# The head products of a group norm as two rounded passes, in newly ordered steps of a two-layer fp32 kernel

## The reference

```
xa = _ln(x, ln1_w, ln1_b)
sx = concatenate([state[:, 1:2] - xa[:, :1], xa[:, :-1] - xa[:, 1:]], axis=1)
xxx = tanh((xa + sx * maa_x) @ maa_w1) ...      # five mixes of xa and sx
w = exp(-exp(time_decay + tanh(xw @ td_w1) @ td_w2))
r, k, v = xr @ Wr.T, xk @ Wk.T, xv @ Wv.T;  g = silu(xg @ Wg.T)
for each token:                                  # the recurrence
    a = k_t[..., :, None] * v_t[..., None, :]
    out = einsum('bhi,bhij->bhj', r_t, u * a + s)
    s = a + w_t[..., :, None] * s
og = out.reshape(b, l, h, s_)                    # group norm over each head's 16 channels
m = og.mean(-1, keepdims=True)
va = ((og - m) ** 2).mean(-1, keepdims=True)
og = ((og - m) / sqrt(va + 1e-05)).reshape(b, l, e) * gn_w + gn_b
x1 = x + og * g @ Wo.T
xc = _ln(x1, ln2_w, ln2_b)
...
return x1 + rr * (kk @ Wfv.T)                    # rr = sigmoid(xr2 @ Wfr.T), kk = relu(xk2 @ Wfk.T)^2
```

## Time and profile before

| | us |
|---|---|
| median of 3 runs | 1405.7 |
| lowest and highest | 1401.32, 1408.68 |
| the profiled execution, its own time | 1402.65 |
| its span, from the first to the last instruction | 1400.8 |
| PE busy | 1331.3 (95% of the span) |
| DVE busy | 928.5 (66%) |
| ACT busy | 734.7 (52%) |
| POOL busy | 489.8 (35%) |

### The profile page before, as it was taken

How to read it: one execution, slowest core, us unless ns; L and a number is a source line. 1 busy time by engine, 2 the same in 40 slices (tenths; PEclk the granted TensorE clock), 3 DMA queues, 4 the chain that set the end, 5 groups by cost and what they waited for, 6 DMA issues and landing times.

```text
span 1400.8 us, 42823 instructions
## 1 busy us (share of the span) xinstructions
PE 1331.3 (95%) x17120; PEld 937.6 (67%) x17120; DVE 928.5 (66%) x2431; ACT 734.7 (52%) x1772; POOL 489.8 (35%) x550
## 2 busy tenths in 40 slices
PE   6999999999999999897899999999999999999977
PEld 5777777777777777666566666766676667666624
DVE  3555555555555555547677877787888888887862
ACT  4776677767667667632425453445345434444332
POOL 3222111222222222113346445543555345534540
PEclk9999999999999999988999999999999999999979
DMA  7333222222222223113000010001010110010000
GB/s 228 99 106 106 93 75 63 74 73 71 61 76 74 75 69 101 54 57 122 22 21 14 23 28 21 15 22 28 22 27 9 28 27 22 10 26 22 15 14 14
DMA packets 39529, 73.70 MB, mean 53 GB/s; under 512 B 17797, under 2 KB 20485, under 8 KB 37829
## 3 DMA queue, kind: packets, MB, share of 16 engines
q1 hardware_dynamic: 39365, 71.24, 17.2%
HBM read 60.24 MB, written 7.57 MB: 48 GB/s over the span
## 4 chain that ended last, share of the span: by engine, by line
PE 82%; DVE 8%; issue 6%; DMA 2%; ACT 1%; SPq 1%; POOL 0%; DVEq 0%; ACTq 0%; POOLq 0%
PE b_bank L1831 18%; PE b_bank L1837 12%; PE ring_bank L703 7%; PE ring_bank L704 6%; PE ring_bank L705 6%; PE av_bank L789 4%; PE b_bank L1945 4%; PE score_banks L762 4%; DVE probs L450 3%; PE b_bank L1982 3%; PE score_banks L749 3%; PE b_bank L1971 2%; PE b_bank L1885 2%; DVE probsT L467 2%; PE av_bank L775 2%
## 5 line engine op out<-in xcount | busy, mean ns | idle before, releaser
L1126 POOL TENSOR_TENSOR rst<-rp,st 128x448 f32<-128x448 f32 x192 | 209.7, 1115 | 55.9 <-DVE st L1349 53.9
L450 DVE CUSTOM_DVE_ANT_0 probs<-score_banks,unmask 112x375 f32<-112x375 f32 x256 | 124.8, 544 | 93.0 <-issue 93.0
L595 ACT ACTIVATE probs<-probs,least_inv 112x375 f32<-112x375 f32 x256 | 152.4, 606 | 32.5 <-DVE least_inv L450 32.5
L467 DVE SCALAR_TENSOR_TENSOR probsT<-score_banks,least_cols 125x448 f32<-125x448 f32 x192 | 107.9, 617 | 53.9 <-PE score_banks L762 51.7
L610 ACT ACTIVATE probsT<-probsT,key_mask 125x448 f32<-125x448 f32 x192 | 114.5, 661 | 47.4 <-DVE probsT L467 47.2
L1118 POOL TENSOR_TENSOR xm<-mixed,xa 128x448 f32<-128x448 f32 x80 | 88.0, 1102 | 145.3 <-DVE mixed L1278 140.0
L340 POOL TENSOR_TENSOR aT_lo<-whole,aT_hi 128x375 fp32r<-128x375 f32 x64 | 59.0, 921 | 152.3 <-ACT whole L576 150.2
L375 POOL TENSOR_TENSOR ctx_rstd<-ctx_var_eps,a_eps_exp 125x3 f32<-125x3 f32 x16 | 13.8, 865 | 272.6 <-DVE ctx_var_eps L423 272.6
L703 PE MATMUL ring_bank<-aT_hi,wk_lo 128*128 128x376 f32 x256 | 91.2, 356 | 0.2 <-issue 0.2
L1628 ACT COPY key<-b_bank 128x448 f32<-128x448 f32 x16 | 8.5, 533 | 148.4 <-PE b_bank L1831 148.4
L704 PE MATMUL ring_bank<-aT_lo,wk_hi 128*128 128x376 f32 x256 | 85.5, 334 | 0.0
(11 more groups left out here) (183 smaller groups left out, 3109.0 us busy)
## 6 DMA issues: line engine op xcount, KB each, us to landing
least_cols<-values_of_two_batches SPq DMA_DIRECT2D x32, 437.5 KB
ctx_tok<-in_ctx SPq DMA_DIRECT2D x16, 672.0 KB
xT_sb<-in_xT SPq DMA_DIRECT2D x16, 224.0 KB, 2.9
inv_cols<-values_of_two_batches SPq DMA_DIRECT2D x128, 28.0 KB, 3.9
x_tok<-in_x SPq DMA_DIRECT2D x16, 224.0 KB, 2.7
x_between_layers<-x_tok SPq DMA_DIRECT2D x16, 224.0 KB, 4.7
b_x<-x_between_layers SPq DMA_DIRECT2D x16, 224.0 KB, 3.0
x_post<-x_between_layers SPq DMA_DIRECT2D x16, 224.0 KB, 2.9
```

The source lines that it names most:

```text
L450: dve.tensor_tensor_reduce(out=probs[:, g % 2, i], in0=score_bank[0:T, i, 0:TC], in1=unmask[:, m[1]], scale=-SCALE, scalar=-LOWEST, op0=AL ...
L467: dve.scalar_tensor_tensor(out=probsT[:, g % 2, k].rearrange("p (i t) -> p i t", t=T), in0=score_bank[0:TK, :, k * T:(k + 1) * T], scalar= ...
L595: act.activation(probs[:, g % 2, i], probs[:, g % 2, i], ACT.Exp, scale=-1.0, bias=least_at(m, g, i), accum_out=sums[:, g, i:i + 1]).then_ ...
L1126: pool.tensor_tensor(by_chunk(rst[:, j % NPROD]), by_chunk(rp[:].rearrange("p c t -> p (c t)")), state_of(j), ALU.mult).then_inc(s_pprod, 1)
```

## The change

Four things change, all in the second phase.

1. **The head products.** `centring` is the identity less the head mean, and `mean_r` the head mean, both as fp32r (a rounded form that takes PE fewer passes). `norm_high` on ACT writes `wkv` rounded, `norm_low` on POOL the rest, `wkv` less the rounded part; `gn_centre` multiplies `centring` by both, which gives the centred values in PSUM at once, and `centre` on DVE is gone. In the same way `square` writes the squares, `square_high` the rounded squares, `square_low` the rest, and `gn_var` has two products.
2. **The SP queue.** In a step: the next input's load, then the spreading of the values of batch m (it stood at the end of the step before, as that of batch n), the store, then `x_post`'s load, which waits for `s_fin` where it waited for `s_x2`.
3. **Memory.** `x2` shares `x_post`, `fin` shares `ln2_tok` (with the waits that this needs), and some constants share a semaphore.
4. **The orders.** Steps 1 and 2 keep about their old order (`early_step`); from step 3 on the order is new on all engines.

```diff
-        def gn_mean(l):
-            pe.wait_ge(s_wkv, count(l, 1, 1))
+        def gn_centre(l):
+            pe.wait_ge(s_gnlo, count(l, 2, 1))
...
-            pe.matmul(norm_bank(l)[0][:, 0:CT], headmean[:], wkv[:].rearrange("p c t -> p (c t)"), start=True,
-                      stop=True).then_inc(s_mean, 1)
+            low, high = (x.rearrange("p c t -> p (c t)") for x in norm_parts(l))
+            pe.matmul(norm_bank(l)[0][:, 0:CT], centring[:], high, start=True, stop=False)
+            pe.matmul(norm_bank(l)[0][:, 0:CT], centring[:], low, start=False, stop=True).then_inc(s_cen, 1)
...
+            low, high = (x.rearrange("p c t -> p (c t)") for x in (norm_parts(l)[1], wkv_r[:]))
+            pe.matmul(norm_bank(l)[1][:, 0:CT], mean_r[:], high, start=True, stop=False)
+            pe.matmul(norm_bank(l)[1][:, 0:CT], mean_r[:], low, start=False, stop=True).then_inc(s_var, 1)
...
+        def norm_low(l):
+            pool.wait_ge(s_gnhi, count(l, 2, 1))
...
+            low, high = norm_parts(l)
+            pool.tensor_tensor(low, wkv[:], high.bitcast(F32), ALU.subtract).then_inc(s_gnlo, 1)
+
+        def square_low(l):
+            pool.wait_ge(s_sq, count(l, 1, 1))
+            pool.wait_ge(s_gnhi, count(l, 2, 2))
+            pool.tensor_tensor(norm_parts(l)[1], norm_home(l)[1], wkv_r[:].bitcast(F32), ALU.subtract).then_inc(s_gnlo, 1)
...
+        def norm_high(l):
+            act.wait_ge(s_wkv, count(l, 1, 1))
...
+            act.copy(norm_parts(l)[1], wkv[:]).then_inc(s_gnhi, 1)
+
         def square(l):
             act.wait_ge(s_cen, count(l, 1, 1))
...
+        def square_high(l):
+            act.wait_ge(s_cen, count(l, 1, 1))
+            act.activation(wkv_r[:].rearrange("p c t -> p (c t)"), norm_bank(l)[0][:, 0:CT], ACT.Square).then_inc(s_gnhi, 1)
...
-        def centre(l):
-            dve.wait_ge(s_mean, count(l, 1, 1))
...
         def group_norm(l):
             dve.wait_ge(s_grs, count(l, 1, 1))
             centred, inverse = norm_home(l)
-            dve.tensor_tensor(centred, centred, inverse, ALU.mult).then_inc(s_gnorm, 1)
+            flat = "p c t -> p (c t)"
+            dve.tensor_tensor(centred.rearrange(flat), norm_bank(l)[0][:, 0:CT], inverse.rearrange(flat), ALU.mult).then_inc(s_gnorm, 1)
...
         def step(n, pre, scan, post):
             m = later(n, -1)
-            if post:
-                l = later(n, -2)
-                if at_least(l, 1):
-                    sp.wait_ge(s_x2, count(later(l, -1), 1, 1))
-                sp.dma_start(x1p[:], A["x1"][index(l)]).then_inc(s_x1p[l[1]], 16)
             if pre and not is_batch(n, B - 1):
                 load_x1(later(n, 1))
+            if scan and not is_batch(n, 1):
+                spread_value(m)
             if post and at_least(n, 3):
                 store_out(later(n, -3))
-            if pre:
-                spread_value(n)
+            l = later(n, -2)
+            if post and not is_last(l):
+                if at_least(l, 1):
+                    sp.wait_ge(s_fin, count(later(l, -1), 1, 1))
+                sp.dma_start(x1p[:], A["x1"][index(l)]).then_inc(s_x1p[l[1]], 16)
```

More of the change, by code:

```diff
@@ L1156, in last_steps @@
             rec_key(m)
+            norm_low(l)
+            square_low(l)
             product(m, 0)
@@ L1170, in last_steps, with early_step @@
             rstd2(l)
+            norm_low(m)
+            square_low(m)
             gate_output(m, False)
             rstd2(m)
[L1174 to L1178, removed]
+        def early_step(n, pre, scan, post):
             p, m, l, more = later(n, 1), later(n, -1), later(n, -2), pre and not is_batch(n, B - 1)
-            early = is_batch(n, 1) or is_batch(n, 2)
-            if more and not early:
-                rstd1(p)
             if scan:
@@ L1187, in step @@
                 mix(n, 1)
-            if early:
                 rstd1(p)
+            if post:
+                norm_low(l)
+                square_low(l)
             if scan:
@@ L1218, in step @@
                 xa_state(p)
+        def step(n, pre, scan, post):
+            if is_batch(n, B):
+                return last_steps()
+            if is_batch(n, B + 1):
+                return
+            if is_batch(n, 1) or is_batch(n, 2):
+                return early_step(n, pre, scan, post)
+            p, m, l, more = later(n, 1), later(n, -1), later(n, -2), pre and not is_batch(n, B - 1)
+            if post:
+                norm_low(l)
+            if scan:
+                rec_key(m)
+            if pre:
+                mix(n, 0)
+            if post:
+                square_low(l)
+            if pre:
+                mix(n, 1)
+            if scan:
+                product(m, 0)
+                product(m, 1)
+            if more:
+                rstd1(p)
+            if scan:
+                product(m, 2)
+            if post:
+                gate_output(l, scan)
+            if pre:
+                mix(n, 2)
+                mix(n, 3)
+            if scan:
+                product(m, 4)
+                product(m, 5)
+                product(m, 6)
+                product(m, 8)
+            if post:
+                rstd2(l)
+            if pre:
+                mix(n, 4)
+            if scan:
+                product(m, 9)
+            if more:
+                xa_state(p)
+            if scan:
+                product(m, 10)
+                product(m, 12)
+                product(m, 13)
+                product(m, 14)
         def rest():
@@ L1751, in last_steps @@
             square(l)
+            square_high(l)
             gn_rstd(l)
             gn_affine(l)
+            norm_high(m)
             square(m)
+            square_high(m)
             xc_affine(l)
@@ L2094, in step @@
                 attend_near(m, 0)
-            if pre and not early:
-                project(n, 1, "wv", s_vmm)
-            if scans:
                 attend_near(m, 1)
                 attend_near(m, 2)
-            if pre and not early:
-                decay_first(n)
             if pre:
```

309 lines of the change are left out of this document (240 added, 69 removed).

## The result

The changed kernel takes 1398.62 us (median of 15 runs, 1396.4 to 1404.51) against 1405.37 for the kernel before (15 runs beside it): a ratio of 0.9964, 95% interval 0.9953 to 0.9976. One of the 15 runs of before took 4009.25 us; the ratio leaves it out, and the other 14 lie between 1399.84 and 1408.68. The forecast was 1394: of its 11.7 us, 6.8 came by the medians and 5 by the ratio. I read durations and waits from the traces and the total from the medians.

The account below looks back on a forecast made before the run. PE was taken to set the pace in 13 steps: -0.83 us each is -10.8, with step 2's -1.2 and the tail's +0.9 -11.1, from 1402.65 to 1391.5; 2 added gives 1394 us, range 1387 to 1409.

Parts of the forecast that it names:

- Head products: Mean and variance products on PE: each 0.95 us fp32 product becomes an fp32r pair of 0.56, saving 0.78 us a step.
- The gap: PE's 0.48 us idle before `maa_second(n, (2, 3, 4))` goes, as `decay_first` stands earlier; 0.45 us a step counted.
- The loss on PE: The last part of `maa_first` and `reduce(m, 3)` no longer run interleaved on PE: +0.2 us a step.
- The allowance: +0.2 us a step for `reduce(m, 0)` and `project_out` on PE, which come within 0.1 us of their time.
- Copies and subtractions: Two added passes each on ACT and POOL, `centre` gone from DVE: `rec_key` and variance product covered, 0.3 to 0.6 us spare.
- SP: SP's queue: next input's load ahead of spreading the values, `x_post`'s load behind the store; covered, moved waits have over 5 us.
- What comes close: At `attend_near(m, 3)` and `project_out`: DVE's `product(m, 3)` and POOL's `product(m, 2)` ready within 0.1 us; if DVE's first, PE never waits.
- rival 1: POOL starts first, the fourth value product stalls PE 1.2 us each step; about 1405, 1407 beside the mean; chance 0.30.
- my case without a wait: The main case: DVE's `product(m, 3)` starts first and nothing on PE waits for the fourth product; 1394 us, chance 0.45.
- the sum: Steady steps 3 to 15: -0.78 - 0.45 + 0.2 + 0.2 = -0.83 us a step, times 13 = -10.8 us.
- The steps ahead: Step 2: chunk sums go ahead of the wait on `wkv`, and the variance product is shorter: -1.2 us.
- The tail: The last batch's norm has nothing beside it; its added copy and subtraction show about +0.9 us at the end.

Follow-up runs that it names:

- near_values_first: The changed kernel with one swap on DVE, `near_values(m, 1)` ahead of `product(m, 3)`: 1413.95 us, ratio 1.0084 to the kernel before.

## Why the prediction was wrong

*Head products*: right. 0.77 us saved a step, 0.78 predicted.

*The gap*: it closed, as predicted (0.48 us gone, 0.45 counted). The reason given, the place of `decay_first`, was only part of it: the tanh's place on ACT had to move too, and in the old orders even both together only moved the wait, as the two runs on the kernel before show.

*The loss on PE*: 0.2 predicted; the run with both interleaved again shows 0.14. Start to start each of the two pieces takes 0.89 us alone, 1.78 together, against the 1.64.

*The allowance* of 0.2 us a step for what is just in time at `reduce(m, 0)` and `project_out`: nothing of it was used. With POOL's order repaired the step is 45.96 - 0.77 - 0.48 + 0.14 = 44.85, which is what the trace has.

*Copies and subtractions*: the cover predicted for `rec_key` and `square_low` was there; from the fourth step on PE waits for neither until the last scan's step, where the variance pair waits 1.50 us for `square_low`.

*SP*: no cost, right. But I called the old place harmless from the old times of its neighbours; with the new ones a load behind the spreading costs some 70 us (1460.76 for 1388.15).

***What comes close***: this is the step that failed. It says that DVE's `product(m, 3)` and POOL's `product(m, 2)` become ready within 0.1 us, and "If DVE's starts first, the fourth product ends at +13.8 and nothing on PE waits". I took that as the likeliest (0.45 against 0.30 for rival 1). The two were ready 0.07 us apart, and POOL's was first. Rival 1's chain then ran as written: the product ends 0.49 behind POOL's (0.47 predicted), the addition meets the gate, PE waits. The wait was 0.99 instead of 1.2 us. Its time, 1405 to 1407, was too high because the wait was shorter and came 12 times and not 13 (11.0 us where 13 x 1.2 is 15.6), and because step 2 gave more. That the meeting with POOL's product is the cause is shown by the run that exchanges it with `rstd1` and changes nothing else: the wait is gone, and the time is 12.6 us (by the ratio) to 14.4 us (by the medians) below that of before, where my case without a wait had 11.7. So of the 10.8 us that the sum expects from the steady steps, 0.5 came (45.92 for 45.96 in 12 steps), and 1.1 more in the one step without the wait. That the total still moved more than half of the way is luck: it has most of its gain from step 2, below.

The Trainium skill, "SBUF — State Buffer", section "SBUF: two separate sides", has whichever of the two operations starts first keep the shared port pair for its whole length, while the other is blocked fully. The traces agree that one is held until the other ends: 1.38 and 1.91 us for an operation of 0.62. That the one that is recorded first wins, they show in most rows, but not in the earlier trace rows.

*The steps ahead*: step 3 starts 3.5 us earlier (734.00 for 737.46), where I had 1.2 for step 2. 0.65 of it comes from the first phase. Step 1 is 1.7 us longer, and step 2 is 4.4 us shorter (51.89 for 56.31). Of these, 2 us are `project_out`, which ran 5.66 us before and 3.60 after; from `maa_second` to its end the granted clock is 0.59 before and 1.00 after. That is not one trace's clock alone: the three traces with the old step 2 have 56.3, 57.3 and 60.0 us for it, and the ten with the new one (two of them with fp32 head products) 51.2 to 54.8. The slow `project_out` is in all three of the old ones and in two of the ten new ones, the two at 54.8. So where `project_out` is slow in both, the new step 2 is 1.5 us shorter (54.8 for 56.3), near the 1.2 of the sum; the rest of the gain of step 2 goes with the clock. Whether the new order keeps the clock up there is not shown, only that the two come together. The trace of before has the shortest of the three old steps, and this would account for part of what the medians show and the two traces don't; the rest of that stays open.

*The tail*: +0.9 predicted. From the last transposes of the chunk keys to `ffn_key(l)` it was 34.62 us and is 35.45, +0.83. The trace then shows another 1.7 at the last key projection, which the clock took. The two traces add up so: 3.46 us from the steps ahead, 0.45 from steps 3 to 14 and 1.11 from step 15, less 0.83 here and 1.39 after it, is the 2.80 between the spans. The last key projection after, and then before (windows, with the columns of the earlier trace rows; the granted clock is the figure ahead of the last two):

```profile
1381.70:1387.00 5.30, 5.26 (x65) 4.94 (x66) 0.97 (x4) 0.26 (x1) 0.00 (x0) 0.68 0.01 3
```

```profile
1386.20:1390.00 3.80, 3.78 (x66) 3.39 (x67) 0.94 (x4) 0.45 (x1) 0.00 (x0) 1.00 0.02 4
```

After, PE spent part of the projection at 1.2 GHz and took 4.95 us for it; before, at a clock of 1.00 throughout, 3.29. Both had idled 3.31 us ahead of it. In the runs of the study this projection took 3.29, 4.95 or 6 us, so it says little of the change, and a difference of 2 us between single traces can be this alone.

## What to carry to other kernels

Where two engines that hold one another become ready within a tenth of a microsecond, the order of start could not be forecast here, and even the recorded starts do not always tell who is held; look for the cheapest edit that pulls the two apart, and treat the case without the wait as half a case at most. Follow such a meeting to the next one too: here the first cost nothing by itself where the second went well, and the 1 us hung on an addition recorded 0.04 us behind the gate. A gap on the engine that sets the pace may be where other engines catch up: closing it in the kernel before made that kernel slower, and the gain came only with the new orders. A wait can cost more than its length: where the granted clock fell after it, 1.6 us of waiting cost 3.3. And the worth of an issue's place on a queue is to be judged with the new times of what stands before and behind it, not with the old.

## What was not expected of the hardware

A waiting VectorE operation is sometimes let in between two back-to-back GpSimd operations (0.86 us for 0.62, and GpSimd's next 0.93 for 0.57) and sometimes held through both (1.91 us). Recorded 0.11 us ahead of a GpSimd operation it was still the one held, recorded 0.15 ahead it was not. An fp32r pair of 448 columns takes 0.61 us start to start as the centring and 0.52 as the variance product, at granted clock 1.00. Two groups of products with weights of 32 columns each run partly beside one another when their calls are neighbours (1.64 us for both, 0.89 each start to start when apart). A wait of 1.6 us on TensorE was followed by a granted clock of 0.74 in some steps and of 1.00 in others of the same run (`near_values_first`).
